# Cross-attention and expert FFN on one core: the last key tile's exponentials summed by TensorE with ones

## What is computed

```python
scores = einsum('bthd,bshd->bhts', q, k) / sqrt(HEAD_DIM)
attn   = softmax(scores, axis=-1)                 # over the 512 keys
update = einsum('bhts,bshd->bthd', attn, v)
```

## Time and profile before

| | |
|---|---|
| median of 3 runs | 1065.43 us (1065.13 to 1066.44) |
| profiled execution, span from first to last instruction | 1056.2 us |
| its own time outside the span | not given; the median less the span is 9.2 us |
| TensorE matmuls busy | 1012.5 us, 96% |
| VectorE busy | 647.5 us, 61% |
| ScalarE busy | 465.9 us, 44% |
| GpSimd busy | 389.0 us, 37% |
| chain of work that ended last | TensorE 91%, VectorE 4%, ScalarE 2% |

### The profile page before, as it was taken

One profiled execution on the slowest core, in us unless ns is written; L12 is line 12 of the kernel. 1 busy time (PEld: TensorE's weight loads), 2 busy tenths in 40 slices (PEclk: granted clock), 3 DMA queues, 4 the chain that ended last, 5 costly groups with the idle time before them and its releaser, 6 DMA issues.

```text
span 1056.2 us, 14941 instructions
## 1 busy us (share of the span) xinstructions
PE 1012.5 (96%) x5198; PEld 773.3 (73%) x5198; DVE 647.5 (61%) x1469; ACT 465.9 (44%) x865; POOL 389.0 (37%) x355
## 2 busy tenths in 40 slices
PE   4789999999999998899999999999999999999998
PEld 3656767676767665567888888888888888888886
DVE  5877777877777557355565555555555555555544
ACT  3346565656665646545323323333333333332322
POOL 3379797879797967345210010010010100100000
PEclk9899999999999999999999999999999999999999
DMA  7343433434333223324222121121220230221220
GB/s 239 104 131 78 131 81 111 108 84 131 73 110 75 65 65 105 92 86 131 75 80 61 52 80 50 61 81 40 72 80 31 71 90 20 91 80 31 93 68 20
DMA packets 65674, 87.87 MB, mean 83 GB/s; under 512 B 10720, under 2 KB 31088, under 8 KB 65600
## 3 DMA queue, kind: packets, MB, share of 16 engines
q1 hardware_dynamic: 63680, 84.83, 28.0%
q10 hardware_dynamic: 1920, 2.10, 0.6%
HBM read 56.97 MB, written 4.46 MB: 58 GB/s over the span
## 4 chain that ended last, share of the span: by engine, by line
PE 91%; DVE 4%; ACT 2%; SPq 1%; issue 1%; DMA 1%; POOL 0%; DVEq 0%; ACTq 0%
PE ps L653 50%; PE pst L653 18%; PE ps L732 6%; PE ps L759 5%; PE pst L748 5%; PE ps L659 4%; PE ps L772 1%; DVE mx L1201 1%; ACT e_buf L868 1%; SPq L606 1%; PE ps L811 1%; SPq L541 1%; ACT ctx_h L868 0%; DVE wsrc_l L1148 0%; PE ps L812 0%
## 5 line engine op out<-in xcount | busy, mean ns | idle before, releaser
L653 PE MATMUL ps<-x_h,weights 128*128 128x512 f32 x1088 | 365.6, 397 | 1.4 <-DVE x L1194 0.8
L653 PEld LDWEIGHTS ps<-x_h,weights 128*128 128x128 f32 x1088 | 204.5, 188 | 51.8 <-issue 1.0
L1201 DVE TENSOR_REDUCE mx<-ps 128x1 f32<-128x512 f32 x256 | 173.3, 685 | 81.8 <-PE ps L732 80.9
L868 ACT ACTIVATE hh<-qb 128x512 fp32r<-128x512 f32 x136 | 86.0, 632 | 296.4 <-DVE qb L1315 273.7
L653 PE MATMUL ps<-x_l,weights 128*128 128x512 f32 x544 | 214.6, 395 | 0.0
L653 PE MATMUL pst<-hh,weights 128*128 128x512 f32 x544 | 194.6, 399 | 0.0
L1304 DVE TENSOR_TENSOR qb<-ps,sg 128x512 f32<-128x512 f32 x136 | 94.1, 692 | 160.2 <-PE ps L653 153.8
L868 ACT ACTIVATE e_buf<-pst 128x512 f32<-128x512 f32 x256 | 147.4, 596 | 92.8 <-PE pst L748 81.8
L1317 DVE TENSOR_TENSOR hl<-qb,hh 128x512 fp32r<-128x512 f32 x136 | 94.3, 693 | 95.0 <-ACT hh L868 95.0
L1407 POOL TENSOR_TENSOR e_sums<-e_sums,e_buf 128x1024 f32<-128x1024 f32 x60 | 143.5, 2391 | 7.2 <-ACT e_buf L868 1.2
L1359 POOL TENSOR_SCALAR ve<-mv 128x4 f32<-128x4 f32 x8 | 1.8, 226 | 347.1 <-DVE mv L1242 347.1
(11 more groups left out here) (159 smaller groups left out, 1391.5 us busy)
## 6 DMA issues: line engine op xcount, KB each, us to landing
cb<-combine_scratch SPq DMA_DIRECT2D x128, 256.0 KB, 3.2
q_stack<-q_h SPq DMA_DIRECT2D x128, 64.0 KB, 2.0
k_stack<-k_h SPq DMA_DIRECT2D x124, 64.0 KB, 2.0
ctx_raw<-in_ctxT SPq DMA_DIRECT2D x7, 1024.0 KB, 5.2
q_stack<-q_l SPq DMA_DIRECT2D x64, 64.0 KB, 2.0
out_x<-ob SPq DMA_DIRECT2D x16, 256.0 KB, 2.2
k_stack<-k_l SPq DMA_DIRECT2D x62, 64.0 KB, 2.0
x<-in_x SPq DMA_DIRECT2D x7, 512.0 KB, 6.5
```

The source lines that it names most:

```text
L653: ins = engine.matmul(dst, lhsT, rhs, start=start and n == 0, stop=stop and n == len(terms) - 1)
L868: return engine.activation(dst, src, func, **kw)
L1201: engine.tensor_reduce(MX[:, g % 2, h // 2, h % 2, q:q + 1], bank(step), AX.X, ALU.max).then_inc(sem("max"), 1)
```

## The change

Two GpSimd adds of each group 0 to 14 go: e_add has i = 0 and 1 only, which sum the key tiles 0 to 2. The four matmuls with ones over `e_sums` leave their PSUM bank open, and four more are issued behind them, with the same ones as weights and the exponentials of the key tile 3 of each head as the moving data; they close the sum. TensorE's wait is for the add i = 1 of half 1. ScalarE no longer waits for an add before it overwrites a slot of key tile 3 (it still waits for the burst). The due times of the adds that stay are the same as before.

```diff
@@ -155,8 +155,8 @@
         for a in range(2 if g < NG - 1 else 0):
-            for i in range(3):
-                at(t + (2.7, 2.8, 5.9, 11.2, 14.3, 15.8)[3 * a + i], ("e_add", g, a, i))
+            for i in range(2):
+                at(t + (2.7, 2.8, 11.2, 14.3)[2 * a + i], ("e_add", g, a, i))
@@ -766,11 +766,13 @@
                     elif part == 1:
-                        pe.wait_ge(sem("e_add"), COUNT["e_add", g, 1, 2])
+                        pe.wait_ge(sem("e_add"), COUNT["e_add", g, 1, 1])
                         ps = own_bank(step)
                         for i in range(4):
-                            ins = engine.matmul(ps[32 * i:32 * i + 32, :], ON[:, :], ES[:, i // 2, i % 2, :],
-                                                start=True, stop=True)
+                            engine.matmul(ps[32 * i:32 * i + 32, :], ON[:, :], ES[:, i // 2, i % 2, :], start=True, stop=False)
+                        for i in range(4):
+                            ins = engine.matmul(ps[32 * i:32 * i + 32, :], ON[:, :], EB[:, SLOTS[8 * g + 4 * (i // 2) + 3], i % 2, :],
+                                                start=False, stop=True)
                     ins.then_inc(sem("av"), 1)
@@ -955,7 +957,7 @@
                         act.wait_ge(*burst_done(m // 8, m % 4 // 2))
-                        if m < NU - 8:
+                        if m < NU - 8 and m % 4 < 3:
                             act.wait_ge(sem("e_add"), COUNT["e_add", m // 8, m // 4 % 2, max(m % 4 - 1, 0)])
```

## The result

| | before | after |
|---|---|---|
| median (7 runs each) | 1065.37 us | 1070.87 us |
| lowest to highest | 1059.67 to 1066.44 | 1068.28 to 1073.12 |
| ratio, 95% interval | | 1.0066 (1.0047 to 1.0085) |
| span of the profiled execution | 1056.2 us | 1066.5 us |
| own time of that execution (of its whole launch) | not given | 1068.28 us |

The change makes the kernel slower, by 0.66% or some 7 us. The forecast was 1074.4 us, +9.0 us or 0.84%, with a range of 1071.5 to 1079.3: the sign and, to within the interval, the size of the difference hold; the ratio on the median known when the forecast was made gives 1065.43 x 1.0066 = 1072.5 us, inside the range.

A forecast was written before the change was run, and what follows sets the result against it. TensorE was taken to bound the kernel, busy 96% of the span. New matmuls +12.9 us and the removed stall -3.9 give +9.0 on the 1065.4 us median: 1074.4 us, range 1071.5 to 1079.3.

The forecast's parts named there:

- 15 x 0.86 = 12.9 us: Ones bursts of 15 groups: four new TensorE matmuls each cost 0.86 us, 12.9 us in all, covered by nothing.
- The rival of the second four that stand behind the first four: Ones bursts: new matmuls wait for the old four, 1.04 us per group, total 1077.1 us; chance 0.04.
- 1.06 us: Ones bursts: estimate for four matmuls at the skill's 79% strip efficiency, making the sum 3 us higher; not adopted.
- the 0.84 us of a full matmul: TensorE: estimated time of one full-array float32 matmul of 512 columns at full clock, compared with four strips' 0.86 us.
- The one stall: Second layer norm's start near 387 us: group 13's add delays a row maximum, TensorE waits 2.29 us; removing it saves 3.9.
- The 3.9 forecast: Saving near 387 us: 2.2 of wait plus 0.68, 0.56 and 0.5 of low clock behind it; bounds 0 and 4.3 us.
- The rival in which it stays: Near 387 us: another producer is as late or the wait moves on; 1078.3 us, or some 1076; chance 0.16.
- The margin of 0.05 us: Near 387 us: without the add the matmul could start at 386.95, TensorE itself being late next by 0.05 us.
- The launch has 9.2 us more than that span in the median of the runs, taken as unchanged: Whole launch: 9.2 us added to the predicted span of 1065.2 us to give the forecast time.
- a fall made elsewhere: Waits at 387, 411 and 440 us shift, so clock falls change, some 1.7 us each; 1072.7 or 1076.1; chance 0.18.
- GpSimd's load as a burden on the others: Attention: adds slow VectorE and ScalarE, so TensorE's 11.9 us of waits could go; 1063.0 us; chance 0.05, half-way case 0.05.
- GpSimd, though loaded, is late at one place only: Attention: TensorE's work lies end to end, and GpSimd delays it only at the second layer norm's start.

The follow-up runs named there:

- e2: Kernel before with all 90 adds kept and only the four matmuls over key tile 3 added in groups 0 to 14; ratio 1.0116 (1.0088 to 1.0145).
- e7: Kernel before with the change for half 1 only: 15 adds gone, two more matmuls in each of 15 groups; ratio 1.0127 (1.0102 to 1.0152).
- e3: Changed kernel without its four matmuls over key tile 3, so only the adds are taken away; ratio against before 0.9953 (0.9935 to 0.9971).
- e6: Kernel before with the change made in group 13 alone, 88 adds and four more matmuls in all; ratio 0.9969 (0.9953 to 0.9984).
- e10: Kernel before with the change in group 13 alone, timed once more; ratio 0.9975 (0.9958 to 0.9992).
- e9: Kernel before with group 13's add i = 2 of half 0 issued behind GpSimd's first Newton step, all 90 adds kept; ratio 0.9970 (0.9957 to 0.9984).
- e1: Kernel before again, no edit; ratio 1.0005 (0.9988 to 1.0022), median 1064.65 us.
- e5: Kernel before with group 13's add i = 2 of half 0 issued behind the layer norm's first two GpSimd steps; ratio 0.9991 (0.9973 to 1.0008).

## Why the prediction held, and where it did not

**TensorE's new work: right.** The step "15 x 0.86 = 12.9 us", not covered by anything, is what e2 shows: +12.3 us (9.4 to 15.4), and 0.86 us a burst in the chains of e2, of the changed kernel and of e7. The rival of the second four that stand behind the first four would have been 1.04 for each; the chain has 0.86.

The Trainium skill's figure for column strips (TensorE: Matmul & The Clock Gate, "Measured speedup vs the span model"), from which I had estimated 1.06 us, is not met here: e7's two strips and the four of the others cost the same 0.86 us, so the strips overlap fully in these float32 matmuls. That rests on e7; the 0.84 us of a full matmul, which the forecast set beside it, is only an estimate, from a stretch whose granted clock was 0.61.

**The one stall: right in place and size.** e3 gives -5.0 us (-6.9 to -3.1) for the adds alone, and for group 13 alone e6 and e10 give -3.3 and -2.7, each with +0.86 of matmuls in it, and e9 gives -3.2. The 3.9 forecast lies inside every interval once the 0.86 is counted, and the traces of e3 and e6 show 3.88 us at the place itself. The rival in which it stays is excluded, by the traces (no wait for a maximum in any of e3, e6, e9, e10) and by the times. The margin of 0.05 us held.

**The sum: right as a difference; one step wrong that did no harm.** The step is "The launch has 9.2 us more than that span in the median of the runs, taken as unchanged". About 2 us lie outside the span (1.8 in the changed kernel's profiled execution, 2.2 in e1's); the other 7 were the distance from an unusually short execution to a typical one. It could not move the forecast: 1056.2 + 9.2 is the median of before again, and 1074.4 is that median plus 9.0. That it cancels was luck; the span of after, 1066.5, plus 9.2 would have missed that execution's own time by some 7 us.

The 3.5 us by which 1070.87 lies below 1074.4 have another source. The median of before stayed where it was (1065.43 with three runs, 1065.37 with seven); it is the difference that came out smaller in this first timing, 7.0 us by the ratio and 5.5 by the medians. The two timings with more runs of before gave 8.9 and 8.5; +9.0 on their medians, 1064.0 and 1062.9, gives 1073.0 and 1071.9, where 1071.98 and 1071.05 were measured. With single runs 5 to 8 us apart, that 1070.87 fell just below the range says little of the mechanism.

**The clock: a spread, not a shift.** In the trace after, the fall behind the wait that was at 411 us and is at 420 now is there again (0.50 from 422 to 426 us), and behind the wait at 450 us the clock stays whole, as behind the one at 440 us in the earlier trace rows. But e1, the kernel before again, has a fall behind its wait at that place, from 443.70 us on. The windows of after (two) and of e1:

```profile
422.00:426.00 4.00, 3.28 (x9) 2.51 (x10) 3.81 (x17) 3.74 (x9) 2.06 (x3) 0.50 0.27 75
...
453.00:458.00 5.00, 5.00 (x37) 1.73 (x38) 0.67 (x2) 2.02 (x5) 1.28 (x1) 1.00 0.12 43
...
443.70:448.10 4.40, 4.40 (x18) 1.37 (x22) 0.79 (x2) 2.04 (x4) 1.28 (x1) 0.50 0.17 55
```

So whether the clock falls there is a matter of the execution, and the 1.00 of the earlier trace rows was that of one. Over the runs of each timing the median granted clock was 0.984 to 0.987 for the kernel before and 0.990 for the changed one, which has one fall fewer: no sign of a fall made elsewhere.

**GpSimd's load as a burden on the others: not in the size of the rival, but my evidence against it was too narrow.** The rival said that all of TensorE's waits would go with a third of the adds; none did but the one. But I argued from a VectorE operation that takes 414 and 413 ns with and without GpSimd's adds, and added that no row has a VectorE operation on two SBUF inputs beside an add. e5 shows an operation that is shut out by an add, and the trace of before has one on two SBUF inputs that is long beside an add, with TensorE's 2.46 us wait behind it (last section). The sentence "GpSimd, though loaded, is late at one place only" is therefore too strong: GpSimd's own steps are late at one place, but at two more the chain to a wait of TensorE runs through a VectorE operation that is long beside an add. Both those adds stay in the changed kernel, and both waits stay.

What stays open: how much of the spread of 8 us between executions of one kernel comes from the clock, and how much from the first 65 us. Two pairs of traces show that both take part. e10 is 2.2 us behind e6, the same kernel, at group 12's burst, with 4.0 us in place of 1.4 at the early wait, and 2.5 behind at the end. e1 is 1.1 us ahead of before at that burst and 4.0 behind at the end, with as much waiting in between and lower clocks behind the waits.

## What to carry to other kernels

Work taken off an engine that is busy at eight tenths is worth only the waits that others have for it, one by one; here, of what the change took away, that was one add of ninety, and reordering or removing that one gave -3 us, where the general version paid 12.9 us of the bounding engine's time for it. A sum over the partitions on TensorE cost the same pass over the moving data with two strips in use as with four (e7), so half of such a change cost as much as all of it. And compare differences with differences: a single profiled span may be 7 us from the typical one, and what is "outside the span" needs a run whose own time and span are both known.

## What the hardware showed that was not expected

**A GpSimd add holds up some VectorE operations until it ends, and not others.** Shown by moving the add: VectorE's tensor-scalar operation on 128x8 elements in SBUF, 2.23 us in place of 0.17, ending 0.03 us after the add (e5); with the add elsewhere it takes 0.17 (e9). The trace of before has further candidates that I had passed over. The first, timeline near 195 us, GpSimd and VectorE:

```profile
195.23 4.89 POOL L1407 TENSOR_TENSOR e_sums<-e_sums,e_buf 128x1024 f32<-128x1024 f32 x2
195.61 2.14 DVE L1229 TENSOR_SCALAR gate_sb<-gate_sb,gate_r 16x256 f32<-16x256 f32 x1
```

A tensor-scalar of 16x256 elements takes 2.14 us, under the first of two adds, and TensorE's 0.9 us wait of the earlier trace rows is for it. It takes 2.17 us in the changed kernel, where one of the adds that remained stands beside it. The second is near 411 us, timeline of GpSimd, VectorE and TensorE:

```profile
410.55 2.35 POOL L1407 TENSOR_TENSOR e_sums<-e_sums,e_buf 128x1024 f32<-128x1024 f32 x1
411.18 1.80 DVE L1267 TENSOR_TENSOR lg<-lg,rn 128x64 f32<-128x64 f32 x1
413.90 0.59 PE L748 MATMUL pst<-q_stack,k_stack 98*128 98x512 f32 x1 [2.46 <-ACT e_buf L868]
```

Line 1267 multiplies two SBUF tiles. This one takes 1.80 us and ends 0.08 us after the add; the seven others of its line, in the experts' part, take 0.22 to 0.23. ScalarE waits 2.43 us for it, with the next exponentials queued behind, and TensorE waits 2.46 for those, with the clock of 0.58 of the earlier trace rows behind the wait. The add is the second of group 14, which stays in the changed kernel: there line 1269 takes 1.81 us at 419.99, and TensorE waits 2.47. If the add is the cause, moving it away would be worth an estimated 1.80 - 0.23 = 1.6 us, and perhaps the fall of the clock behind the wait. No run moved either of these two, so their cause is argued, not shown.

Not held up: the row maxima and the additions that read PSUM (0.68 us beside the add in e9), the statistics of the earlier trace rows (only five of the 64 stood beside an add, with 416 to 418 ns), and tensor-scalar operations of one element a partition (line 1095 of before, 84 of them, none over 0.21 us, many beside adds).

The Trainium skill (Trainium Architecture — The Big Picture, "What this means for kernel authors") calls the port that VectorE and GpSimd share an exclusive lock. e5 and e9 agree for the tensor-scalar operation on 128x8, with 2.23 against 0.17 us; for the operations named as not held up the traces show no exclusion.
